# Low halves of the router weights ahead of GpSimd's rotated sums, and tile 3 turned ahead of the short tile's later sums

## What is computed

```python
h = concat([patchify(x) @ W.T + b, txt], axis=1)      # 32 x 113 x 256
h = h + attention(layernorm(h))                       # 16 heads of 16, rotary q and k, softmax, output projection
z = layernorm(h)                                      # soft mixture of experts, 64 experts x 32 slots
logits = z @ phi_w.T + phi_b                          # 3616 tokens x 2048
D, Cw = softmax(logits, slots), softmax(logits, experts)
X = clip(D.T @ z);  X = tanh(layernorm(X));  Y = X @ expert_w + expert_b
out = h + Cw @ Y
```

## Time and profile before

| engine | busy us | share of the span |
|---|---|---|
| PE | 897.7 | 97% |
| PEld | 745.1 | 81% |
| DVE | 719.5 | 78% |
| ACT | 497.5 | 54% |
| POOL | 535.9 | 58% |

### The profile page before, as it was taken

How to read it: one execution, slowest core, us unless ns; L and a number is a source line. 1 busy time by engine, 2 the same in 40 slices (tenths; PEclk the granted TensorE clock), 3 DMA queues, 4 the chain that set the end, 5 groups by cost and what they waited for, 6 DMA issues and landing times.

```text
span 923.0 us, 21774 instructions
## 1 busy us (share of the span) xinstructions
PE 897.7 (97%) x7668; PEld 745.1 (81%) x7668; DVE 719.5 (78%) x1085; ACT 497.5 (54%) x801; POOL 535.9 (58%) x518
## 2 busy tenths in 40 slices
PE   8989999999999988999999999999999999999997
PEld 7777887888887667888888888888888758888885
DVE  3577777778775789999999999999999765555552
ACT  1255555555554466676766766667666563333331
POOL 1375332232331379999999999999999661010000
PEclk9999999999997989999999999999999999999999
DMA  8601111111111156423233232332336996767660
GB/s 248 217 28 46 44 41 43 40 45 44 44 48 35 34 109 187 131 71 103 65 91 85 69 102 62 91 89 66 104 102 199 385 385 222 236 229 235 230 187 18
DMA packets 99925, 110.98 MB, mean 120 GB/s; under 512 B 12216, under 2 KB 91156, under 8 KB 93860
## 3 DMA queue, kind: packets, MB, share of 16 engines
q1 hardware_dynamic: 97760, 106.23, 37.7%
q0 software_dynamic: 1376, 3.70, 1.1%
q10 hardware_dynamic: 740, 0.41, 0.2%
HBM read 72.06 MB, written 38.21 MB: 119 GB/s over the span
## 4 chain that ended last, share of the span: by engine, by line
PE 87%; POOL 6%; DVE 2%; issue 2%; ACT 1%; DMA 1%; SPq 0%; DVEq 0%; POOLq 0%; ACTq 0%
PE slots_p_sum L1460 21%; PE slots_logits L1492 15%; PE slots_p_turn L1601 11%; PE slots_p_turn L1609 6%; PE attend_p_qk L568 5%; PE slots_p_turn L1445 5%; PE attend_p_row L568 4%; PE attend_p_score L549 3%; PE attend_p_k L560 3%; PE attend_p_score L540 3%; PE embed_acc L148 2%; PE attend_p_qk L577 2%; PE slots_logits L1570 2%; PE attend_p_k L555 1%; PE attend_p_q L555 1%
## 5 line engine op out<-in xcount | busy, mean ns | idle before, releaser
L1460 PE MATMUL slots_p_sum<-slots_x,slots_disp 128*128 128x256 f32 (+1 forms) x928 | 210.3, 384 | 3.0 <-POOL slots_disp L1194 2.7
L1460 PEld LDWEIGHTS slots_p_sum<-slots_x,slots_disp 128*128 128x128 f32 (+1 forms) x928 | 175.1, 192 | 28.6 <-POOL slots_disp L1194 3.9
L1189 POOL TENSOR_TENSOR slots_comb<-slots_comb,slots_cmax 128x1024 f32<-128x1024 f32 x56 | 107.9, 1946 | 5.9 <-DVE slots_cmax L971 3.3
L1601 PE MATMUL slots_p_turn<-slots_y_parts,slots_hi 128*128 128x512 f32 (+1 forms) x464 | 111.0, 391 | 0.0
L446 POOL TENSOR_TENSOR attend_stack<-attend_rope_a,attend_rope_b 113x128 f32<-113x128 f32 x128 | 54.4, 457 | 86.9 <-DVE attend_rope_b L396 86.9
L1240 POOL DMA_DIRECT2D out<-slots_o x29 | 15.9, 547 | 143.5 <-DVE slots_o L1106 143.5
L1201 POOL TENSOR_TENSOR slots_comb<-slots_comb,slots_csum 128x2048 f32<-128x2048 f32 x27 | 97.8, 3623 | 1.6 <-DVE slots_csum L948 1.6
L1601 PEld LDWEIGHTS slots_p_turn<-slots_y_parts,slots_hi 128*128 128x128 f32 (+1 forms) x464 | 84.0, 186 | 18.0 <-DVE slots_lo L1120 0.4
L1194 POOL TENSOR_TENSOR slots_disp<-slots_disp,slots_dsum 128x2048 f32<-128x2048 f32 x27 | 98.5, 3649 | 0.0
L958 DVE TENSOR_TENSOR slots_disp<-slots_logits,slots_dmax 128x512 f32<-128x512 f32 x112 | 77.4, 691 | 4.1
L480 ACT ACTIVATE attend_prob_t<-attend_p_score 113x904 f32<-113x904 f32 x64 | 55.7, 924 | 40.6 <-PE attend_p_score L549 40.6
(11 more groups left out here) (171 smaller groups left out, 1855.4 us busy)
## 6 DMA issues: line engine op xcount, KB each, us to landing
combine_t<-slots_ct SPq DMA_DIRECT2D x224, 128.0 KB, 2.4
slots_comb<-combine_t SPq DMA_DIRECT2D x14, 1024.0 KB, 5.7
slots_ct<-combine_t SPq DMA_DIRECT2D x14, 1024.0 KB, 5.8
slots_spare_w<-wexp SPq DMA_DIRECT2D x6, 1024.0 KB, 6.2
slots_disp<-wexp SPq DMA_DIRECT2D x6, 1024.0 KB, 8.0
expert_w<-wexp SPq DMA_DIRECT2D x4, 1024.0 KB, 10.7
h<-attend_h_out SPq DMA_DIRECT2D x32, 113.0 KB
slots_h_t<-h SPq DMA_DIRECT2D x28, 128.0 KB, 2.3
```

The source lines that it names most:

```text
L1189: nc.gpsimd.tensor_tensor(m, m, cmax[0:rows, shalf(i)].unsqueeze(2).broadcast_to([rows, SLOTS // 2, EXPERTS]), ALU.subtract).then_inc(csub ...
L1460: last = nc.tensor.matmul(p_sum[u % 2][:, i, :], disp[d][part].rearrange("p n s -> p (n s)")[:, 128 * block:128 * block + 128], x[d][part] ...
L1601: return nc.tensor.matmul(p_o[c % 2][0:rows], hi[c % 2][:, e, 0:rows], y_parts[:, e].rearrange("p i c -> p (i c)"), start=e == 0, stop=e = ...
```

## The change

Two edits.

1. POOL's low halves of pieces 0, 1 and 2 move from the end of steps 1, 2 and 3 to between the root and the rotated sums of steps 2, 3 and 4. Piece 3 stays at the end of step 4.
2. In the opening, PE turns tile 3 behind the logits of tile 2 and ahead of the short tile's units 2 to 7, instead of in step 2. ACT keeps its high half between the two exponentials of tile 1's combine weights (it waits there for all logits of tile 2, which read the same buffer), and keeps units 2 to 7 behind the second exponential instead of around it.

```diff
@@ -434,6 +434,12 @@
                 nc.gpsimd.tensor_tensor(mv[:, 1:2], mv[:, 1:2], eps[:], ALU.add).then_inc(var_ok, 1)
                 pool.wait_ge(var_ok, val(b + 4))
                 nc.gpsimd.tensor_tensor(rstd[:], mv[:, 1:2], power[:], ALU.pow).then_inc(rstd_ok, 1)
+            if isinstance(b, int) and 2 <= b <= PIECES:
+
+                i = b - 2
+                pool.wait_ge(phi_hi_ok, i + 1)
+                nc.gpsimd.tensor_tensor(piece(phi_lo, i), piece(phi_raw, i), piece(phi_hi, i).bitcast(F32),
+                                        ALU.subtract).then_inc(phi_lo_ok, 1)
             if projects:
                 pool.wait_ge(rope_ok, val(b + 3))
                 if scores:
@@ -454,7 +460,7 @@
                 part = slice(i * KC * E // PIECES % E, i * KC * E // PIECES % E + KC * E // PIECES)
                 nc.gpsimd.tensor_tensor(piece(phi_raw, i)[rows], piece(phi_raw, i)[rows], phi_drop[rows, part],
                                         ALU.subtract).then_inc(phi_sub_ok, 1)
-            if isinstance(b, int) and 1 <= b <= PIECES:
+            if isinstance(b, int) and b == PIECES:
 
                 i = b - 1
                 pool.wait_ge(phi_hi_ok, i + 1)
@@ -1293,14 +1299,14 @@
                 if not static(t) or t >= RING:
                     act.wait_ge(sum_ok, val(summed_before(t, c)))
                 nc.scalar.activation(x[c % RING][0:rows], xn[c % 2][0:rows, 0:C], ACT.Copy).then_inc(kept_ok, 1)
-            def high_turned():
-                act.wait_ge(xt_ps_ok, val(t + 2))
+            def high_turned(n):
+                act.wait_ge(xt_ps_ok, val(n + 1))
                 if opening:
-                    act.wait_ge(logit_ok, 2 * NB)
+                    act.wait_ge(logit_ok, n * NB)
                 nc.scalar.activation(xt_hi[:, :, 0:nrows], p_turn[0][:, 0:KC, 0:nrows], ACT.Copy).then_inc(xt_hi_ok, 1)
 
-            if nxt and not opening:
-                high_turned()
+            if nxt and not (static(t) and t <= 2):
+                high_turned(t + 1)
             if live:
                 wait_for(act, ct_ps_ok, 4 * (t - 1))
                 for b in range(NB):
@@ -1309,7 +1315,7 @@
                     nc.scalar.activation(comb[c % 2][0:rows, :, bank(b)],
                                          logits[0:rows, bank(b), :].rearrange("p n s -> p s n"), ACT.Copy).then_inc(copied_ok, 1)
                     if opening and b == 1:
-                        high_turned()
+                        high_turned(2)
                     if units and not opening and b == 1:
                         keep_sum(*units[0])
                     if static(t) and t == LAST and b == 1:
@@ -1327,11 +1333,13 @@
             for i in range(2):
                 if live:
                     exp_half(comb[c % 2], shalf, csub_ok, 1, cexp_ok, i)
-                if opening:
-                    for one in (units[PER:2 * PER], units[2 * PER:])[i]:
-                        keep_sum(*one)
+                if opening and i == 0:
+                    high_turned(3)
                 if weights:
                     keep_quarter(t - 1, (c + 1) % 2, half(-1), 2 + i)
+            for one in units[PER:] if opening else []:
+                keep_sum(*one)
+
         def rest(keep_values, high):
 
 
@@ -1496,7 +1504,7 @@
         def step(t, half, c):
             live, nxt, ahead = flags(t)
             nrows = rows_of(t + 1)
-            if nxt and not (static(t) and t == 1):
+            if nxt and not (static(t) and t <= 2):
                 turn_x(t, c, nrows)
             opening = static(t) and t == 1
             multiply_group(t, c, slice(0, PER))
@@ -1509,6 +1517,7 @@
             if nxt:
                 multiply_logits(t, nrows, [2, 3])
             if opening:
+                turn_x(2, 2, 128)
                 multiply_group(t, c, slice(PER, UNITS))
 
         def short_logits(b, columns):
```

## The result

The changed kernel took 935.33 us, the median of four runs from 933.25 to 936.2, against 926.6 for the kernel before, run beside it on the same chip. The ratio is 1.0116, with a 95% interval from 1.0093 to 1.0138. The profiled execution took 933.25 us, with a span of 931.6 us. It was forecast 2.75 us faster and came out some 9 us slower.

A forecast was written before the change was run, and what follows sets the result against it. PE carries 87% of the chain, with POOL the bound in attention steps 2 to 4 and after the mixture's opening. Gains 2.35 + 0.4 = 2.75 us, counted from a mean of 925.3, give 922.6 us, range 919.9 to 926.2.

The forecast's parts named there:

- What bounds the kernel: Attention steps 2 to 4: POOL's queue is the bound, by one low half per step; mixture's opening: start of combine maxima.
- the 2.35 forecast: Attention steps 2 to 4: moving the low halves removes PE stall of 27.07 - 3 x 8.24 = 2.35 us.
- The price not shown: Low half beside DVE's `xn` and rotation products: 0.03 us per step, 0.1 in all, left in the range.
- The rule against the trace: Skill page's blocking of the second engine to start on shared ports: said not to be shown for this shape by one row.
- Slower: Rival: POOL's low half holds up `xn` in steps 2 to 4, 1.35 us each, 4.05 in all; 929.0 us, chance 0.06.
- The sign of being wrong at the end of the prediction: Forecast wrong if the clock is half over a different stretch, at the mixture's opening or the attention's end.
- The pace behind: Attention steps 2 to 4: low half ends near 60.6, then two rotated sums are done at 61.5, before PE's reading at 61.9.
- the forecast cover: Rotated sums done 0.4 us before PE reads them; beyond it, each 0.1 us of longer low half costs PE 0.1.
- Edit 2: Mixture's opening, tile 3 turned early: combine maxima start sooner, worth 0 to 0.7 us with the same clock, taken as 0.4.
- the last unit of the short tile: Mixture's opening: with the clock falling near 327.1 it leaves PE near 332.0, maxima at 335.9, nothing gained.

The follow-up runs named there:

- e6: Kernel before with the low halves at the end of POOL's steps 5 to 8, written out for it, and tile 3 turned early: 919.87 us, ratio 0.9951.
- e3: Changed kernel plus one wait: POOL waits for DVE's `xn` of the same step ahead of each moved low half: 920.9 us, ratio 0.9966.
- e4: Changed kernel with each moved low half cut into four instructions of 256 columns: 922.05 us, ratio 0.9974.
- e1: Kernel before with only the low halves moved, tile 3 left where it was: 935.02 us, ratio 1.0122.
- e5: Changed kernel with PE repeating the turning back of the attention's output ten times in steps 2 to 4, ahead of its wait for `xn`: 928.0 us, ratio 1.0031.
- e9: e6 plus POOL clearing half of phi_lo between root and rotated sums in steps 2 to 4: 925.29 us, a single execution.

## Why the prediction was wrong, point by point

- **What bounds the kernel.** Right: POOL's low half in front of the root was the bound of steps 2 to 4. Taken out of the way of both, it gave what was asked of it: in `e6` PE's steps last 8.18 us and steps 1 to 5 together 2.6 us less than before, against the 2.35 forecast. The place ahead of the sums gave less: 1.65 us in `e3`, 1.4 in `e4`. The medians, 3.9 and 4.9 us under before in `e3` and `e6`, are larger than that and hold other things as well.
- **The price not shown.** This is the step that failed. The prediction took the length of DVE's normalisation in the earlier trace rows, 0.44 us beside a POOL operation, for the price of the two together, 0.03 us per step, and left it out of the sum. The measured price is 2.02 us (2.43 against 0.41). The row did not say what was read from it: the POOL operation there had been at work since 394.03 and ended at 395.30, only 0.29 us behind the start of DVE's at 395.01. What the row shows is DVE waiting out those 0.29 us and ending 0.15 us later. Two more pairs of the kernel before fit, if the ends are compared (timeline, steps of the mixture):

```profile
365.56 1.29 POOL L1150 TENSOR_TENSOR sums_bias<-sums_bias,slots_part_sum 128x512 f32<-128x512 f32 x1
...
366.52 0.48 DVE L931 TENSOR_SCALAR slots_xn<-slots_h_t,slots_mv,slots_rstd 128x256 f32<-128x256 f32 x1
```

```profile
437.11 1.28 POOL L1150 TENSOR_TENSOR sums_bias<-sums_bias,slots_part_sum 128x512 f32<-128x512 f32 x1
...
438.38 0.41 DVE L931 TENSOR_SCALAR slots_xn<-slots_h_t,slots_mv,slots_rstd 128x256 f32<-128x256 f32 x1
```

  In the first POOL's operation ends at 366.85 and DVE's, 0.48 us long, at 367.00, 0.15 us later. In the second it ends at 438.39, DVE starts at 438.38 and needs 0.41, as it does alone. An overlap of 0.3 us hardly shows in the length of DVE's operation; it shows in the ends.
- **The rule against the trace.** The Trainium skill's page "SBUF — State Buffer", section "Who interferes with whom", has the second of the two to start blocked for the whole of the first, and the prediction set that aside on one row. The traces agree with the wait: `xn` waits for the whole of POOL's instruction and no longer (2.43, 1.87 and 0.81 us beside 2.35, 1.80 and 0.73). That `xn` uses both pairs of ports, the page's condition for it, no trace shows.
- **The rival.** "Slower" named the mechanism, its place and 1.35 us per step, 4.05 in all. With PE kept busy the measured price is 3.6 us. But it had 6% and a time of 929.0, and the time came out 6 us over that, because the rival priced an idle PE at its idle time. The 5.5 us of half clock behind it were in no term. The sign of being wrong at the end of the prediction names such a stretch, at other places.
- **The pace behind.** Two sums were to be done 0.4 us ahead of PE. In the changed kernel this can't be seen, since DVE was late itself. In `e3` the sums start 0.8 us later than the 60.6 of the prediction, and the weight loads wait 0.29 us. That is of the size of the forecast cover, and bears out that what goes beyond it shows on PE.
- **Edit 2.** Forecast 0.4 us, between 0 and 0.7 with the same clock; measured 0.8 to 0.9 by the traces, with the clock down as in the profile before, so over the upper bound. Both waits, for the late load and for ACT's copies, showed as told. What was mis-sized is the last unit of the short tile: it was to be kept 1.0 us later than before, which would have used up the whole gain, and came 0.5 us later (8.22 against 7.74).

## What to carry to other kernels

Before an operation of one engine is moved beside one of another with which it never ran, look for any pair of the same kinds in the trace and compare their ends, not their lengths: an operation that ends each time the same short while behind another engine's may have been waiting for it, even where it is just 0.03 us longer than usual. If there is no such pair with a long overlap, price the edit at the full length of the longer one. Two remedies worked here: a wait that keeps the two operations apart, and cutting the long one into pieces. And where an idle stretch of PE is added rather than taken away, price the clock with it; here it cost more than the stretch.

## What the hardware showed that was not expected

- DVE's `tensor_scalar` of 113x256 from SBUF to SBUF, started up to 0.1 us behind a POOL instruction on SBUF, lasts as long as that instruction: 2.43 us beside a subtraction of 2.35, 1.87 beside a clearing of 1.80, 0.81 beside the first of four pieces of 0.73, against 0.41 alone. It ends 0.14 to 0.15 us after POOL's instruction. DVE's products with one operand in PSUM were as long as ever beside the same POOL operation.
- PE's clock was found at half behind idle stretches of 1.9 us in some steps and at full speed in others, with the same attention program: 5.5 us in one execution of the changed kernel, 2.6 in the one of `e1`, none in `e5`, where PE had work in their place. In `e9` it fell once, behind stretches of 1.3 us. The Trainium skill's page "TensorE: Matmul & The Clock Gate", section "What's actually happening", has the clock fall behind idle time. `e5` agrees, with 1.00 in 50 to 90 us; the steps of `e1` that stayed at 1.00 behind 1.9 us, and the fall in the mixture's opening with PE busy 1.66 of 2 us, show that idle stretches alone don't tell when it falls.
- A turn of this hardware loop costs 0.35 us on PE: steps of 8.37 and 8.01 us by turns in the loop, 8.0 written out.
